# A recommendation tower on one core: embedding turns in another order, with a ring of ten rows

## The reference, cut to what matters

```python
combined = jnp.concatenate([sparse_x, dense_x[:, None, :]], axis=1)
interact = jnp.einsum('bfd,bgd->bfg', combined, combined)
return interact[:, _TRIU_I, _TRIU_J]
...
e = jnp.stack([tbl_0[ids[:, 0]], ..., tbl_25[ids[:, 25]]], axis=1)
z = _L0_rec_ref(e, r_dense_x)
z = z.reshape(z.shape[0], -1)
h = jnp.concatenate([z, r_dense_x], axis=1)
h = jnp.maximum(h @ W_top1 + b_top1, 0.0)     # 479 -> 512
h = jnp.maximum(h @ W_top2 + b_top2, 0.0)     # 512 -> 256
y = h @ W_top3                                # 256 -> 1
```

## Time and profile before

| what | value |
|---|---|
| median of 3 runs | 412.77 us (412.57 to 418.06) |
| profiled execution, its time | 414.51 us |
| its span, first to last instruction | 412.7 us |
| mean granted TensorE clock | 0.979 |
| PE busy | 382.2 us, 93% |
| POOL busy | 283.1 us, 69% |
| DVE, ACT busy | 246.2 us (60%), 236.7 us (57%) |
| chain that ended last | PE 66%, POOL 22%, issue 7%, transfers 2% |

### The profile page before, as it was taken

The page is one execution under the profiler, slowest core; times in us unless marked ns, Lnnn a source line. Parts: engine busy times, 40 slices in busy tenths (PEclk is TensorE's granted clock), DMA queues, the critical chain, the costliest instruction groups (busy, mean ns, idle before and its releaser), DMA issues.

```text
span 412.7 us, 8012 instructions
## 1 busy us (share of the span) xinstructions
PE 382.2 (93%) x2976; PEld 355.1 (86%) x2976; DVE 246.2 (60%) x713; ACT 236.7 (57%) x429; POOL 283.1 (69%) x294
## 2 busy tenths in 40 slices
PE   5998989669896999999999999999999999999877
PEld 3888889558895999989999999989999999998766
DVE  6786988527584476827685667637683667133311
ACT  3467735625455465666656665665657655686334
POOL 6777777777777777777777777777777777771000
PEclk9999999959999899999999999999999999999989
DMA  8971231213212213222222223212222222211000
GB/s 210 262 230 51 52 94 54 67 46 89 66 54 68 65 52 85 65 63 68 71 68 69 66 57 85 72 53 64 76 69 67 65 68 70 70 55 49 6 14 2
DMA packets 21637, 30.54 MB, mean 74 GB/s; under 512 B 6960, under 2 KB 15864, under 8 KB 21472
## 3 DMA queue, kind: packets, MB, share of 16 engines
q0 software_dynamic: 9216, 18.89, 16.3%
q1 hardware_dynamic: 12041, 10.91, 10.1%
q10 hardware_dynamic: 343, 0.24, 0.2%
HBM read 26.86 MB, written 0.01 MB: 65 GB/s over the span
## 4 chain that ended last, share of the span: by engine, by line
PE 66%; POOL 22%; issue 7%; DMA 2%; ACT 1%; ACTq 1%; DVE 0%; POOLq 0%
POOL rows L263 22%; PE ps_gram L336 21%; PE ps_mlp L345 15%; PE ps_feat L315 10%; PE ps_feat L317 10%; PE ps_feat L279 6%; PE ps_feat L289 2%; DMA rows<-in_tbl,ids_now 2%; PE ps_mlp L411 2%; PE ps_mlp L352 1%; ACTq L202 1%; DMA ids_now<-in_ids_gathered 1%; PE ps_feat L352 1%; ACT hid L602 0%; POOLq L100 0%
## 5 line engine op out<-in xcount | busy, mean ns | idle before, releaser
L263 POOL DMA_INDIRECT rows<-in_tbl,ids_now x288 | 282.4, 981 | 89.2 <-issue 86.0
L761 DVE TENSOR_SCALAR hot<-ids_all,row_no 125x256 fp32r<-125x256 f32 x512 | 160.2, 385 | 6.0 <-ACT ids_all L558 2.9
L336 PE MATMUL ps_gram<-feat 128*123 128x108 f32 x1024 | 125.3, 278 | 3.3 <-ACT feat L524 3.3
L336 PEld LDWEIGHTS ps_gram<-feat 128*123 128x123 f32 x1024 | 118.2, 192 | 9.2 <-ACT feat L524 5.2
L315 PE MATMUL ps_feat<-hot,table_hi 125*128 125x256 f32 x480 | 117.8, 287 | 1.8 <-ACT stage L540 0.9
L317 PE MATMUL ps_feat<-hot,table_lo 125*128 125x256 f32 x480 | 115.5, 282 | 0.0
L510 DVE COPY z<-ps_gram 27x208 f32<-27x208 f32 x128 | 46.9, 366 | 105.3 <-PE ps_gram L336 102.1
L315 PEld LDWEIGHTS ps_feat<-hot,table_hi 125*128 125x128 f32 x480 | 90.5, 189 | 4.4 <-ACT feat L524 1.5
L317 PEld LDWEIGHTS ps_feat<-hot,table_lo 125*128 125x128 f32 x480 | 90.4, 188 | 0.0
L524 ACT COPY feat<-ps_feat 128x512 f32<-128x512 f32 (+1 forms) x80 | 76.6, 985 | 11.2 <-PE ps_feat L279 10.8
L510 ACT COPY z<-ps_gram 27x208 f32<-27x208 f32 x128 | 41.7, 326 | 55.2 <-PE ps_gram L336 53.5
(11 more groups left out here) (57 smaller groups left out, 319.4 us busy)
## 6 DMA issues: line engine op xcount, KB each, us to landing
rows<-in_tbl,ids_now POOLq DMA_INDIRECT x288, 2.5
table_lo_before<-in_tbl SPq DMA_DIRECT2D x8, 448.0 KB
dense<-in_dense_t SPq DMA_DIRECT2D x8, 128.0 KB
w_lo_before<-in_w SPq DMA_DIRECT2D x1, 1024.0 KB, 16.7
zp_lo_before<-in_dense_t SPq DMA_DIRECT2D x8, 128.0 KB, 2.5
zp_lo_before<-z SPq DMA_DIRECT2D x15, 39.0 KB
zp_lo_before<-z SPq DMA_DIRECT2D x15, 36.0 KB
w_lo_before<-in_w SPq DMA_DIRECT2D x1, 512.0 KB, 18.2
```

The lines of the kernel that those rows point to most:

```text
L263: nc.gpsimd.indirect_dma_start(rows[:, row_at(t, f), :], None, gathered[f], bass.IndirectOffsetOnAxis(ap=ids_now[:, t, f:f + 1], axis=0),) ...
L336: mm = nc.tensor.matmul(ps_gram[at % 2][0:FOUR, c, 0:4 * F], four[:, 0:FOUR], four.rearrange("d (j f) -> d j f", f=FPAD)[:, :, 0:F], start ...
L761: op = nc.vector.tensor_scalar(hot[0:VROWS, u % HOTS, c, :], ids[0:VROWS, k, :], row_no[0:VROWS, no + UNIT * i + c:no + UNIT * i + c + 1], ...
```

## The change

1. `ROWS`, the ring of fetched rows, has 10 slots in place of 30.
2. The order of `even` and `odd` on PE, ACT and DVE: turns stand further apart, the fourth batch of products is between turns 3 and 4 of an even tile, the third batch ahead of turn 1 of an odd one, a block of layer 1 ahead of turn 2.
3. The first half: tile 0's turn 0 stands between the lookups of table 0 and table 1, and the others between later lookups.
4. The ids matmuls contract over 128 partitions, 124 of them zero, instead of 4. DVE zeroes that tile once.
5. The end: the dense part of half 7's layer 1 is computed ahead of half 6's layer 2, in the two `ps_feat` banks and the first `ps_gram` tensor; ACT splits that dense part and finishes half 6's fourth hidden block ahead of its three transfers.

```diff
-ROWS = GATHERED + 12
+ROWS = 10
...
-        ident, ident_r = sb("ident", [P, P]), sb("ident_r", [PAIRS, PAIRS], F32R)
+        ident, ident_r = sb("ident", [P, P]), sb("ident_r", [P, PAIRS], F32R)
...
-            return ps_feat[n - 2] if n in (2, 3) else ps_mlp[at % 2]
+            return ps_feat[n] if n in (0, 1) else last_gram[:, n - 2, :] if n in (2, 3) else ps_mlp[at % 2]
...
+            def last_layer1_dense():
+                h = HALVES - 1
+                pe.wait_ge(zp_lo_ready, h + 1)
+                pe.wait_ge(emptied, len(FEAT_AT))
+                for n in range(HID1 // P):
+                    if n == 2:
+
+                        pe.wait_ge(z_by_act, BATCHES * TILES - 1)
+                        pe.wait_ge(z_by_dve, BATCHES * TILES - 1)
+                    three(OUTS * h + n, w1_hi, w1_lo, zp_hi, zp_lo[h % 2], n, ZP_CHUNKS - 1, True, False)
+
...
@@ PE, even(t) @@
                 turn(t, 1)
                 products(t - 1, 2)
                 spread_ids(h + 1, 0)
-                products(t - 1, 3)
+                turn(t, 2)
+                layer2(h - 3, 0)
                 spread_ids(h + 1, 1)
                 look_up(h, 3)
-                turn(t, 2)
-                layer2(h - 3, 0)
                 turn(t, 3)
+                products(t - 1, 3)
                 turn(t, 4)
                 layer2(h - 3, 1)
@@ PE, odd(t) @@
                 turn(t, 0)
                 products(t - 1, 1)
                 layer3(h - 3)
+                products(t - 1, 2)
                 turn(t, 1)
-                products(t - 1, 2)
                 spread_ids(h + 1, 2)
                 products(t - 1, 3)
+                layer1(h - 2, 0)
+                turn(t, 2)
                 look_up(h + 1, 0)
-                turn(t, 2)
-                layer1(h - 2, 0)
+                layer1(h - 2, 1)
+                turn(t, 3)
                 spread_ids(h + 1, 3)
-                layer1(h - 2, 1)
+                layer1(h - 2, 2)
                 look_up(h + 1, 1)
-                turn(t, 3)
-                layer1(h - 2, 2)
                 turn(t, 4)
                 layer1(h - 2, 3)
@@ PE, tile 0 @@
-            for n in range(PAIRS):
-                look_up(0, n)
-                turn(0, n)
-            turn(0, PAIRS)
+            look_up(0, 0, slice(0, 1))
+            turn(0, 0)
+            look_up(0, 0, slice(1, 2))
+            turn(0, 1)
+            look_up(0, 1)
+            turn(0, 2)
+            turn(0, 3)
+            look_up(0, 2)
+            turn(0, 4)
+            look_up(0, 3)
@@ PE, the end @@
             layer1(h, 3)
+            last_layer1_dense()
             layer2(h, 0)
@@ ACT, the end @@
+            act.wait_ge(packed_dense[(h + 1) % 2], 16 * ((h + 1) // 2 + 1))
+            act.wait_ge(mlp_done, OUTS * h + HID1 // P)
+            split_zp(h + 1, slice(ZP_CHUNKS - 1, ZP_CHUNKS))
+            result1(h, 3)
             pack_rects(act, TILES - 1, range(LAST_BY_SP, len(RECTS)))
-            result1(h, 3)
             result2(h, 0)
-            result2(h, 1)
-
-            act.wait_ge(packed_dense[(h + 1) % 2], 16 * ((h + 1) // 2 + 1))
-            split_zp(h + 1, slice(ZP_CHUNKS - 1, ZP_CHUNKS))
             zp_packed(TILES - 2)
             split_zp(h + 1, slice(0, ZP_CHUNKS - 1), slice(0, P))
-            store_y(h)
+            result2(h, 1)
             zp_packed(TILES - 1)
             split_zp(h + 1, slice(0, ZP_CHUNKS - 1), slice(P, HALF))
+            store_y(h)
@@ DVE, even(t) @@
                 take(t - 1, 2)
-                take(t - 1, 3)
                 put_dense(t)
                 build(h + 1, 0)
+                take(t - 1, 3)
                 rest_zp(h - 2)
@@ DVE, the start @@
+            nc.vector.memset(ids_few_no[:].bitcast(F32), 0.0).then_inc(constants_set, 1)
```

71 lines of the change are left out of this document (32 added, 39 removed).

## The result

| | before | changed |
|---|---|---|
| median | 412.67 us (410.64 to 418.06, 4 runs) | **421.63 us** (421.19 to 423.71, 4 runs) |
| profiled execution, its span | 414.51, 412.7 us | 421.6, 419.8 us |
| mean granted clock | 0.979 | 0.996 |
| last gather starts | 372.19 | 383.65 |
| from there to the end of the span | 40.5 us | 36.2 us |

The changed kernel takes 1.022 times as long (95% interval 1.016 to 1.028). The forecast was 413.3 with a range up to 419.5, so it was wrong: the time lies 2.1 us above the range. The last two lines of the table already say where. The end became shorter by 4.3 us, close to the 4.5 of the forecast. GpSimd's last gather came 11.5 us later, where 5 were forecast, and 11.5 - 4.3 is, rounded, the 7.1 us between the two spans.

A forecast was written before the change was run, and what follows sets the result against it. The prediction took two equally long chains, PE's and POOL's gathers, to bound the kernel up to tile 15, so any POOL loss shows at the end. 412.8 + 5.0 (ring) - 4.5 (end) = 413.3 us, range 408 to 419.5.

The forecast's parts named there:

- The end (-4.5): After the last products, dense part ahead of layer 2: the end starts 4.5 us earlier, bounds -3 and -4.8.
- The ring in the halves with layers (4.4): Ten slots stall POOL before group 3 of even tiles 6 to 14, 0.8 to 0.9 us each, 4.4 in all.
- my loop: Even tile's turn 1, through POOL's gathers to odd tile's turn 2, along PE to next turn 1: 46.3 us against 45.5.
- The ring at the start (0.5): Gather 26 must wait for tile 1's turn 0, which ended at 39.44 before the change: 0.5 us, once.
- Tile 0's turns and the ids: First 37 us: turn 0 in time for gather 8, ids matmuls at the same pitch, zeroing hidden: 0, bounds -0.5 to +1.
- I expect it by then: At the start: tile 0's turn 0 ends before gather 8 starts at 13.37, so no time is lost.
- the ring's term: The cost of ten slots, start and halves with layers together: +5 us, between +3 and +8.
- Never dry: Rival: the ring never stalls POOL and only the end's gain is left, 408.3 us; chance 0.17.
- the clock falls: Rival: PE's waits in each half lower its clock, six places on the loop cost 9.9 us, 423.2; chance 0.10.
- It decides from waits of some 2 us: From the clock rival: PE's clock falls behind waits of some 2 us; those forecast mid-kernel are below 1 us.
- The ring costs twice as much: Rival: slower slot release and PE's waits for ACT make each half lose 1.9 us, 418.3 us; chance 0.12.

The follow-up runs named there:

- run 3: The changed kernel with the ids matmuls over 4 rows again, without the zeroed tile and ACT's wait for it: 421.57 us, 1.023 of the kernel before.
- run 2: The changed kernel with four slots in place of three for the copied ids (`ids_all`): 420.70 us, 1.019 of the kernel before.
- run 5: The changed kernel, ring of ten, with tile 0's lookups and turns ordered as in the kernel before: 538.45 us, beside 614.41 for the kernel before.

## Why the prediction was wrong

**The end (-4.5): right**, in size and by its steps; measured -4.3 to -4.4. Of these 1.8 us are layer 2's 24 matmuls alone (4.65 to 2.89 us): no long wait stands ahead of them now, and the granted clock over them is 1.00 (404.36 to 407.20) where it was 0.63 (393.60 to 398.20).

**The ring in the halves with layers (4.4): right in mechanism, its size partly by luck.** Seven waits of 0.3 to 0.9 us, 4.3 us in all, before group 3 of even tiles; those of tiles 6 to 14 give 3.5, and tiles 2 and 4 the other 0.8, where I had laid out none. PE's waits in tile 7, ended by gathers, stand before turn 0 and before turn 2; I had only the second:

```profile
183.28 0.66 PE L280 MATMUL ps_feat<-ident,rows 128*128 128x128 f32 x4 [1.13 <-DMA rows<-in_tbl,ids_now]
...
193.20 0.66 PE L280 MATMUL ps_feat<-ident,rows 128*128 128x128 f32 x4 [0.80 <-DMA rows<-in_tbl,ids_now]
```

That the sum fits is partly luck: it was worked out with an ids pitch of 0.42, and a kernel with that pitch (run 3) waits for 0.7 to 1.1 us in each. And the waits are not the whole price. A half takes 46.5 us of GpSimd in the changed kernel (168.77 to 215.30, 46.3 by my loop), but from gather 84 to gather 264 it loses 6.1 us against the kernel with 30 slots, 1.2 in each of five halves. 3.5 of them are waits; the rest is gathers that lasted longer, for which no term stood in the forecast.

**The ring at the start (0.5) and "Tile 0's turns and the ids", which ends in "All 0; bounds -0.5 to +1 together": this failed.** Measured, the waits up to gather 26 are 6.5 us. "Turn 0 must end before gather 8 starts, at 13.37" was right; "I expect it by then" was a guess, though the trace had rows for it: turn 0 ran at 16.15 to 16.75 in the kernel before, and 22 more gathers could go out there before the first wait for a turn. None of what makes it late was priced: the first lookup's new place in the bank order (4.2 us by the rows, 3.7 in run 2); the table load behind an added wait (1.4 us, run 3); the 6.5 us of the first 16 matmuls, which would make gather 8 late by 0.8 us even from the old start of the lookup; and the landing, for which I took 2.41 us from a quiet stretch where the first 30 us of the kernel before have a median of 7.6. Run 2 shows that the landing is the next to bind as soon as the lookup is early. By run 5 the same ring costs more with the old start: 7.8 us of waits up to gather 12 against 6.2. So the missed amount belongs to the ring's term, not to the move of tile 0. With gather 26 I had the right turn (38.84) but took its time from before, and PE reaches it at 44.80 now.

**The rivals.** "Never dry" is false. So is "the clock falls" for the loop: the mean clock rose to 0.996, and behind waits of 1.13 and 0.80 us the turns took 0.66 us, as the one of 2.00 did in the earlier trace rows. The one fall stands in a half without layers, as in the earlier trace rows: behind a wait of 2.34 us the turn at 100.52 took 1.11 us at a granted clock of 0.50. The length of the wait alone doesn't decide it, as I had it ("It decides from waits of some 2 us"): behind one of 2.73 us the turn at 53.93 took 0.66.

```profile
53.93 0.66 PE L280 MATMUL ps_feat<-ident,rows 128*128 128x128 f32 x4 [2.73 <-DMA rows<-in_tbl,ids_now]
...
100.52 1.11 PE L280 MATMUL ps_feat<-ident,rows 128*128 128x128 f32 x4 [2.34 <-DMA rows<-in_tbl,ids_now]
```

The Trainium skill describes waits for data that throttle PE in each round of a loop ("TensorE: Matmul & The Clock Gate", section "HAM oscillation — how this bites in real kernels"); the loop of the halves with layers shows no such fall. "The ring costs twice as much" came nearer in size (418.3, still 3.3 us short) but has the wrong place: it put all of the added price into the loop of each half, and 6 of the 8 us that were missed lie in the waits before gather 26.

**What stays open.** The changed kernel is 9.0 us slower by the medians and 7.1 by the spans; the kernel before's profiled execution was 1.8 above its median. Between kernels the gathers' own busy time differs by up to 3.7 us (279.5 in run 3, 283.2 in the changed kernel), which shifts the last gather without any wait. What stretches single gathers from 0.95 to 2.0 us wasn't tested. In the changed kernel all six of more than 1.7 us overlap a subtraction on DVE (L759), but 37 gathers of at most 1.0 us overlap one too, so an overlap alone doesn't do it. What the new order of turns and the cheaper ids matmul do by themselves is open as well: no run with 30 slots has the one without the other, and together they come to about nothing there (408.5 measured, 412.7 - 4.4 = 408.3 by the end alone). How many slots are enough, and what made the kernels with 10 to 14 slots 9 to 17% faster than the kernel before at the times when that took over 600 us, is open too.

## What to carry to other kernels

Before shortening a ring, write down for each of its first uses when the slot must be free and read in the trace when its reader ran: cover that nobody counts hides a late start, and here a PE late by 5.7 us made no gather wait with 30 slots, and 6.5 us of waits stood up to gather 26 with ten. Take a transfer's duration from the stretch in which it will be waited for. When several kinds of work share banks in a fixed order, moving one changes whose copy every later one waits for; and when two engines' chains are of equal length, work saved on one can come back as a wait on the other, so a fix must be judged at the last instruction of the chain, not at the wait that it removes.

## What the runs showed of the hardware

- A gather of 64 KB lands 2.5 us after issue in the median from 100 to 380 us, and 7.6 us in the first 30 us of the kernel before, while another queue holds 72.9% of the 16 DMA engines.
- A slot freed by PE starts the waiting gather 0.27 us later (19.39 to 19.66 in the changed kernel, 15.98 to 16.25 in run 2). With twelve and fourteen slots gather 12 started 0.4 to 2.3 us after the turn; why is open.
- An ids matmul of the same 512 columns costs PE 0.27 us less when it contracts over 128 rows than over 4: the products ahead of it pass on after 1.64 us in place of 1.80, and it passes on itself after 0.32 in place of 0.43 (by the rows of run 3 and of the changed kernel). I had expected no difference. Why it is so wasn't tested.
- ACT's table load took 1.28 us at 1.17 when the landing of the ids was all that the cast waited for (the kernel before, run 3), and moved behind the landing, to 3.16, when another wait was added in front (the changed kernel).
- In the changed kernel 16 matmuls of a first lookup took 6.5 us from 12.27, and 16 more of the same shape 3.45 us from 19.23, both at a granted clock of 1.00. Why wasn't tested.
